# Windowed attention in units of four head pairs, with the value product turned around

## The reference

```python
x = attn_layer(shift_tokens(x), Wqkv[i], ...) + x      # 16 heads of 64
x = ffn_layer(shift_tokens(x), ...) + x
# in attn_layer
q, k, v = split(x @ Wqkv)
q, k = l2norm(q) * qs, l2norm(k) * ksc                  # then rotary tables
sim = einsum('bhwie,bhwje->bhwij', bq, bk2) * 8.0       # windows of 32, look back one window
attn = softmax(where(mask, -big, sim), -1)
out = einsum('bhwij,bhwje->bhwie', attn, bv2)
return out @ Wo
```

## Time and profile before

| what | us |
|---|---|
| median of three runs | 3748.63 (3744.89 to 3750.44) |
| the profiled execution, its own time | 3743.95 |
| its span | 3742.1 |
| TensorE busy | 3470.4 (93%) |
| VectorE busy | 3141.4 (84%) |
| ScalarE busy | 2271.7 (61%) |
| GpSimd busy | 1852.4 (50%) |

### The profile page before, as it was taken

One profiled execution on the slowest core, in us unless ns is written; L12 is line 12 of the kernel. 1 busy time (PEld: TensorE's weight loads), 2 busy tenths in 40 slices (PEclk: granted clock), 3 DMA queues, 4 the chain that ended last, 5 costly groups with the idle time before them and its releaser, 6 DMA issues.

```text
span 3742.1 us, 161812 instructions
## 1 busy us (share of the span) xinstructions
PE 3470.4 (93%) x63907; PEld 2773.6 (74%) x63907; DVE 3141.4 (84%) x6016; ACT 2271.7 (61%) x4159; POOL 1852.4 (50%) x1604
## 2 busy tenths in 40 slices
PE   5758999999999999999999999999999999999996
PEld 2326787877788878788878788877788887788784
DVE  8987888888788888788888788888788888888883
ACT  2014666666666666666666666666566666666663
POOL 2435455454554554545554445545455445455541
PEclk9988999999999999999999999999999999999998
DMA  2002423323333323333223333232432332332332
GB/s 84 9 28 50 104 60 70 77 54 78 91 67 77 72 56 80 82 77 77 64 64 76 85 77 71 57 77 67 95 72 59 73 77 54 79 74 60 70 77 73
DMA packets 186363, 261.00 MB, mean 70 GB/s; under 512 B 31670, under 2 KB 89908, under 8 KB 185396
## 3 DMA queue, kind: packets, MB, share of 16 engines
q1 hardware_dynamic: 186164, 258.24, 30.7%
HBM read 22.30 MB, written 4.19 MB: 7 GB/s over the span
## 4 chain that ended last, share of the span: by engine, by line
PE 71%; issue 13%; DVE 7%; POOL 3%; ACT 3%; SPq 2%; DMA 1%; ACTq 0%; POOLq 0%; DVEq 0%
PE bank L653 9%; PE bank L705 8%; PE bank L637 7%; PE bank L613 6%; PE obank L687 6%; PE bank L738 5%; PE bank L615 4%; PE bank L614 4%; PE bank L697 4%; PE bank L663 4%; PE bank L745 3%; DVE xs_lo L1139 3%; PE bank L647 2%; PE bank L628 2%; PE bank L630 2%
## 5 line engine op out<-in xcount | busy, mean ns | idle before, releaser
L951 POOL TENSOR_TENSOR qn<-qn,rinv 128x512 f32<-128x512 f32 x768 | 805.4, 1065 | 1382.1 <-DVE rinv L1198 1382.1
L945 POOL TENSOR_TENSOR qn<-ropec,ropes 128x512 f32<-128x512 f32 x768 | 982.9, 1294 | 274.6 <-DVE ropes L1150 230.8
L1149 DVE TENSOR_TENSOR ropec<-bank,rots 128x512 f32<-128x512 f32 x768 | 526.7, 686 | 116.0 <-ACT sq L833 63.7
L1158 DVE TENSOR_REDUCE ss<-sq 128x8 f32<-128x512 f32 x768 | 513.2, 679 | 88.0 <-ACT sq L833 82.6
L1150 DVE TENSOR_TENSOR ropes<-bank,rots 128x512 f32<-128x512 f32 x768 | 523.7, 682 | 0.0
L833 ACT ACTIVATE sq<-bank 128x512 f32<-128x512 f32 x768 | 448.8, 598 | 87.7 <-PE bank L615 68.9
L855 ACT ACTIVATE Pr<-Pr 128x512 f32<-128x512 f32 x384 | 241.9, 630 | 399.1 <-DVE Pr L1209 396.9
L637 PE MATMUL bank<-ident,qn 128*128 128x128 f32 x3072 | 464.1, 274 | 18.4 <-POOL qn L951 14.9
L653 PEld LDWEIGHTS bank<-kT,qT 64*32 64x32 f32 x24576 | 363.1, 107 | 122.0 <-issue 121.9
L613 PE MATMUL bank<-wqkv_hi,xs_hi 128*128 128x512 f32 x768 | 353.1, 460 | 99.2 <-DVE xs_lo L1139 90.8
L637 PEld LDWEIGHTS bank<-ident,qn 128*128 128x128 f32 x3072 | 375.9, 141 | 83.9 <-issue 18.8
(11 more groups left out here) (137 smaller groups left out, 6215.9 us busy)
## 6 DMA issues: line engine op xcount, KB each, us to landing
V<-Vt SPq DMA_DIRECT2D x576, 260.0 KB
V<-Vt SPq DMA_DIRECT2D x192, 130.0 KB
V<-Vt SPq DMA_DIRECT2D x192, 65.0 KB
xres<-X SPq DMA_DIRECT2D x96, 128.0 KB
X<-x SPq DMA_DIRECT2D x96, 128.0 KB, 2.0
wqkv_raw<-L_ffn_Wqkv SPq DMA_DIRECT2D x6, 1536.0 KB
xraw<-X SPq DMA_DIRECT2D x97, 64.0 KB
xraw<-X SPq DMA_DIRECT2D x97, 63.8 KB
```

The costliest lines, as they stand in the source:

```text
L945: pool.tensor_tensor(qn[:, c, :], ropec[:, c % ROPE_RING, :], ropes[:, c % ROPE_RING, :], ALU.add).then_inc(rope_sum.sem, 1)
L951: pool.tensor_tensor(heads8(qn[:, c, :]), heads8(qn[:, c, :]), rinv[:, 8 * c:8 * c + 8].unsqueeze(2).broadcast_to([P, 8, DH]), ALU.mult).t ...
L1149: dve.tensor_tensor(halves(ropec[:, c % ROPE_RING, :]), raw, table(t, 2 * kind), ALU.mult)
L1158: dve.tensor_reduce(ss[:, 8 * c:8 * c + 8], heads8(sq[:, c % 2, :]), AX.X, ALU.add).then_inc(ss_done.sem, 1)
```

## The change

1. A unit of attention is now 128 queries and four head pairs (8 heads) rather than every second head. The scores of the two heads of a pair lie in the two halves of the rows and go to two banks (`b_sim` is now the first 256 columns of both banks of `pair`); the mask matmul becomes two of 256 columns.
2. The value product has V as the stationary side, in strips of 32 of the 64 head columns, and PT as the moving side (32 columns): 64 matmuls a unit rather than 32, and its output (`b_o`, the other 256 columns of both banks) is already transposed. Step `ot` goes from TensorE; ScalarE copies `b_o` to OT.
3. The softmax sum no longer comes from a column of ones. VectorE sums Pr and takes the reciprocal (step `rs`), and GpSimd scales Pr ahead of the transpose (step `pn`). VectorE's step `pv` goes.
4. Scores and value product share the two banks, so each of them waits for the reader of the one before (`pair_free`). The freed bank makes the projection banks three.
5. The V moves are issued in two groups, 8 and 10 transfers, for the two halves of the tokens. Wo's rows are loaded in the matching order.
6. The written-out order of all four engines is new.

```diff
-V_DMAS = 10
+V_DMAS = [8, 10]
 ORDER = {
     "pe": """
-        tr.0' pt.2'' w1.0''' pv.1'' proj.0 proj.1 tr.1' ot.0'' w1.1''' tr.2' pv.2'' pt.3'' tr.3' proj.2
-        proj.3 tr.4' ot.1'' w1.2''' tr.5' pv.3'' proj.4 ot.2'' tr.6' w2.0''' ot.3'' tr.7' proj.5 proj.6
-        qk.0' wo.0'' qk.1' proj.7 v.0 mean.0'' pt.0' qk.2' var.0'' pt.1' pv.0' qk.3' v.1 v.2 ln.0'' v.3 """,
+        w1.0''' pt.1'' tr.1' proj.0 proj.1 proj.2 w1.1''' tr.2' pv.1'' tr.3' w1.2''' proj.3 proj.4 proj.5
+        tr.4' pt.2'' w2.0''' tr.5' pv.2'' tr.6' pt.3'' proj.6 tr.7' pv.3'' proj.7 qk.0' wo.0'' qk.1' v.0
+        pt.0' mean.0'' qk.2' v.1 var.0'' v.2 pv.0' v.3 ln.0'' qk.3' tr.0 """,
     "act": """
...
+        xs.0 wa.1 wa.2 tr.0' w1.0''' proj.0 tr.1' proj.1 pt.1'' w1.1''' tr.2' proj.2 ot.1'' tr.3' w1.2'''
+        wc.2''' proj.3 qk.3'' tr.4' pt.2'' proj.4 tr.5' proj.5 ot.2'' tr.6' pt.3'' proj.6 tr.7' ot.3''
+        proj.7 qk.0' x1.0'' wc.0'' v.0 pt.0' mean.0'' qk.1' v.1 ot.0' v.2 v.3 qk.2' ln.0'' wc.1'' wc.3''' """,
     "dve": """
...
+        rs.2'' xs.0 wa.1 wa.2 qk.3'' w1.0''' proj.0 sums.0 sums.1 w1.1''' proj.1 proj.2 sums.2 w1.2'''
+        proj.3 rs.3'' sums.3 w2.0''' sums.4 proj.4 proj.5 sums.5 sums.6 proj.6 qk.0' proj.7 rs.0' x1.0''
+        qk.1' sums.7 mean.0'' qk.2' var.0'' rsqrt.0 rs.1' ln.0'' """,
     "pool": """
...
+        norm.3' add.0 norm.4' norm.5' add.1 add.2 norm.6' pn.3'' norm.7' add.3 add.4 pn.0' add.5 add.6
+        norm.0 pn.1' norm.1 pn.2' add.7 norm.2 """,
 }
-        obank = ps("obank", [P, 2, 512])
-        b_proj, b_trA, b_trB, b_sim, b_c = bank[0:2], bank[2], bank[3], bank[4], bank[5]
+        pair = ps("pair", [P, 2, 512])
+        b_proj, b_trA, b_trB, b_c = [bank[0], bank[1], bank[4]], bank[2], bank[3], bank[5]
+        b_sim = pair[:, :, 0:4 * 2 * WIN]
+        b_o = pair[:, :, 4 * 2 * WIN:512]
             def b_qk(b, u):
...
+                pair_free("qk", b, u)
+                for par in range(2):
+                    pe.matmul(b_sim[:, par, :], identb[:], maskb[:, 1 if t else 0, :].unsqueeze(1).broadcast_to([P, 4, 2 * WIN]),
+                              start=True, stop=False, skip_group_check=True)
+                for j in range(4):
                     for w in range(4):
+                        for par in range(2):
+                            rows = slice(64 * par, 64 * par + 64)
+                            q0 = t * P + w * WIN
+                            mm = pe.matmul(b_sim[w * WIN:(w + 1) * WIN, par, j * 2 * WIN:(j + 1) * 2 * WIN],
+                                           qT[rows, 4 * mh + j, q0:q0 + WIN],
+                                           kT[rows, 4 * mh + j, q0:q0 + 2 * WIN],
+                                           start=False, stop=w == 3 and j == 3, skip_group_check=True)
+            def pair_free(kind, b, u):
+                at = PAIR_ORDER.index((kind, u))
+                k, n = PAIR_ORDER[at - 1]
                 batch = b if at else b - 1
+                if k == "qk":
+                    hold(pe, pe_held, sim_shift.sem, sim_shift.at(batch, n + 1))
                 else:
+                    hold(pe, pe_held, ot_copied.sem, ot_copied.at(batch, n + 1))
             def b_pv(b, u):
...
+                for w in range(4):
+                    for jj in range(2):
+                        wg = 4 * t + w
+                        for odd in range(2):
+                            j = 2 * jj + odd
+                            for dh in range(2):
+                                for par in range(2):
+                                    rows = slice(64 * par, 64 * par + 64)
+                                    strip = 32 * (2 * (par ^ odd) + dh)
+                                    mm = pe.matmul(b_o[strip:strip + 32, odd, jj * P + w * WIN:jj * P + (w + 1) * WIN],
+                                                   V[rows, wg // 2, wg % 2, 4 * mh + j, 32 * dh:32 * dh + 32],
+                                                   PT[rows, u % 2, j * P + w * WIN:j * P + (w + 1) * WIN],
+                                                   start=True, stop=True, skip_group_check=True)
-            def b_ot(b, u):
-                pe.wait_ge(on_done.sem, on_done.at(b, u + 1))
-                trB_free(b, "ot", u)
-                for j in range(4):
-                    mm = pe.transpose(b_trB[:, j * P:(j + 1) * P], On[:, u % 2, j * P:(j + 1) * P], ident[:])
-                mm.then_inc(trB_full.sem, 1)
+            def b_pn(b, u):
+                pool.wait_ge(rs_done.sem, rs_done.at(b, u + 1))
+                pool.tensor_tensor(heads8(Pr[:, u % 2, :]), heads8(Pr[:, u % 2, :]),
+                                   rs[:, u % 2, :].unsqueeze(2).broadcast_to([P, 8, 2 * WIN]), ALU.mult).then_inc(p_scaled.sem, 1)
-            def b_pv(b, u):
-                dve.wait_ge(o_full.sem, o_full.at(b, u + 1))
...
+            def b_rs(b, u):
+                dve.wait_ge(p_ready.sem, p_ready.at(b, u + 1))
+                dve.tensor_reduce(rsum[:, u % 2, :], heads8(Pr[:, u % 2, :]), AX.X, ALU.add).then_inc(rsum_done.sem, 1)
+                dve.wait_ge(rsum_done.sem, rsum_done.at(b, u + 1))
+                dve.reciprocal(rs[:, u % 2, :], rsum[:, u % 2, :]).then_inc(rs_done.sem, 1)
```

More of the change, by code:

```diff
@@ L246, in build @@
         v_copied = per_batch("v_copied", 4)
-        v_placed = per_batch("v_placed", 16 * V_DMAS)
+        v_placed = [per_batch(f"v_placed_{t}", 16 * V_DMAS[t]) for t in range(2)]
         trA_full = per_batch("trA_full", 8)
@@ L409, in load_weights @@
                 sp.dma_start(wqkv_raw[:], Wqkv[one].rearrange("l p n -> p (l n)")).then_inc(w_in_sem, 16)
-                for slot in range(2):
+                for odd in range(2):
                     for par in range(2):
-                        src = Wo[one].rearrange("l (j s r p) n -> s r p (l j) n", j=4, s=2, r=2)[slot, par]
-                        sp.dma_start(wo_raw[slot * 64:slot * 64 + 64, 4 * par:4 * par + 4, :], src).then_inc(w_in_sem, 16)
+                        src = Wo[one].rearrange("l (i o r p) n -> o r p (l i) n", o=2, r=2, p=64)[odd, par]
+                        half = 64 * (par ^ odd)
+                        sp.dma_start(wo_raw[half:half + 64, odd::2, :], src).then_inc(w_in_sem, 16)
                 sp.dma_start(w1_raw[:], W1[one].rearrange("l p n -> p (l n)")).then_inc(w_in_sem, 16)
@@ L446, in load_x, with place_v, move @@
                 sp.dma_start(xraw[64:P, 1:T], X[64:P, bass.ds(g * T, T - 1)]).then_inc(x_loaded.sem, 16)
[L448 to L468, removed]
+            def place_v(n, t):
+                hold(sp, sp_held, v_copied.sem, v_copied.at(n, 2 * t + 2))
+                hold(sp, sp_held, o_full.sem, o_full.at(n - 1, 2 * t + 2))
+                for par in range(2):
+                    half = 64 * par
+                    def move(dst, w, odd, src, rows, tile=t):
+                        d = V[dst:dst + rows, 2 * t + w, odd].rearrange("p m c -> p (m c)")
+                        v = Vt[src:src + rows, tile, par].rearrange("p m c -> p (m c)")
+                        sp.dma_start(d, v).then_inc(v_placed[t].sem, 16)
+                    move(half, 0, 1, 0, 64)
+                    move(half, 1, 1, 64, 64)
+                    move(half, 1, 0, WIN, 64)
+                    move(half + WIN, 0, 0, 0, WIN)
+                    if t == 1:
+                        move(half, 0, 0, P - WIN, WIN, tile=0)
             def body(n, g, lags, layer, c_layers, conv_c=None):
@@ L533, in _ @@
             for m in range(3):
-                mm = pe.transpose(b_sim[:, m * P:(m + 1) * P], la_w_rows[:, m, :], ident[:])
+                mm = pe.transpose(bank[4][:, m * P:(m + 1) * P], la_w_rows[:, m, :], ident[:])
             mm.then_inc(la_wt, 1)
@@ L593, in la_output @@
                 for t in range(4):
[L594 removed]
+                    mm = pe.matmul(pair[:, 1, t * P:(t + 1) * P], la_y[:, t * P:(t + 1) * P], la_w[:, 3, :], start=True, stop=True)
                 mm.then_inc(la_po.sem, 1)
@@ L640, in b_qk @@
             def b_qk(b, u):
-                t, par = UNIT[u]
+                t, mh = UNIT[u]
                 if u == 0:
                     pe.wait_ge(trA_copied.sem, trA_copied.at(b, 8))
[L645 to L649, removed]
-                    for w in range(4):
[L651 to L656, removed]
+                pair_free("qk", b, u)
[3 more added lines that the diff above has]
+                for j in range(4):
+                    for w in range(4):
+                        for par in range(2):
[5 more added lines that the diff above has]
+                                           start=False, stop=w == 3 and j == 3, skip_group_check=True)
                 mm.then_inc(sim_full.sem, 1)
             def b_pt(b, u):
-                pe.wait_ge(p_ready.sem, p_ready.at(b, u + 1))
-                trB_free(b, "pt", u)
+                pe.wait_ge(p_scaled.sem, p_scaled.at(b, u + 1))
+                pe.wait_ge(pt_copied.sem, pt_copied.at(b, u) if u else pt_copied.at(b - 1, 4))
```

(10 more changed lines are left out.)

110 lines of the change are left out of this document (47 added, 63 removed).

## The result

| kernel | median us | ratio to before, 95% interval |
|---|---|---|
| before | 3748.8 | |
| changed | 4531.6 | 1.208 (1.205 to 1.211) |

The account below looks back on a forecast made before the run. TensorE's steps, one after the other, times 96 batches plus one wait, were taken as the bound. Terms -167 - 92 + 12 + 204 - 91 + 85 = -49 us took 3744 to 3695, stated as 3690, range 3550 to 3830.

Parts of the forecast that it names:

- The value product: TensorE, turned-around product: 64 added instructions at 8.2 to 8.7 ns, +0.53 us a unit, +204 us (+115 to +346).
- Scores in eight places: TensorE, score matmuls: a unit falls from 1.03 to 0.79 us, -92 us over 384 units.
- The transposes: TensorE, line 697: the four output transposes of each unit disappear, 0.435 us each time, -167 us.
- The wait for xs_lo: TensorE, ahead of a batch's first projection: the whole 90.8 us wait is credited, -91 us (0 to -91).
- The wait for the roots: TensorE at ln.0'': new wait for the reciprocal roots, 0.85 us a batch, +85 us (0 to +150).
- The shared banks: Scores and value product wait for the previous reader; thinly covered, costed at nothing (-5 to +40 us).
- GpSimd: Four added scalings of 4.3 us raise it from 17.3 to 21.6 of 34 us a batch, just hidden.
- VectorE: Second limit: no difference in its work, 29.3 us a batch still fits in TensorE's about 34.0.
- Transfers: V moves, 10 to 18 issues a batch: up to 0.7 us late for ScalarE's copy, costed at nothing.
- A: Value product: small instructions cost 12.9 to 14.0 ns, +317 to +346 us, so 3808 to 3837 us; chance 0.18.
- B: Value product: the two row halves exclude each other in a bank, +442 instead of +204, 3933 us; chance 0.08.
- C: VectorE or the softmax chain sets the pace: waits of 0.5 us a batch, +48, back to 3743; chance 0.13.

Follow-up runs that it names:

- e7: The changed kernel with the value product in strips of 64 in units 0 and 2, of 32 in units 1 and 3: 3718.8 us, 0.993.
- e1: The changed kernel with the value product in two strips of 64 instead of four of 32, half the instructions: 3661.9 us, 0.978.
- e3: The changed kernel with each row half of the value product writing into its own bank: 4570.7 us, 1.219.
- e4: The kernel before with the value product issued twice in the last two of four units: 3932.9 us, 1.049.
- e6: The kernel before with the value product issued twice in the last three of four units: 4363.8 us, 1.165.
- e9: The code of e4 with 128 idle semaphore increments ahead of the layers: 4064.5 us, 1.083.
- e5: The kernel before with the value product issued twice by a two-turn hardware loop around one copy of its code: 4096.9 us, 1.094.

## Why the prediction was wrong

**What bounds the kernel.** "So the time is the sum of TensorE's steps, one after the other, times 96 batches, plus one wait" was right in the main for the kernel before and for the kernels here whose code is held. It is the sentence that failed for the changed one: the steps are still what I said, but TensorE is not given the instructions in time. I had no rival for it. What could have warned me stands in the page of before: q8, 138 packets, nearly all of them near the changes of layer. These are the 15 packets of 100 us there; between 1600 and 1800 us, in mid-layer, there is none:

```profile
q8 instruction: 15, 0.25, 1.1%
```

So the loop's code was held, and holding it must have a limit. My stretch of 34.55 us lay at such a change of layer, too; in mid-layer a batch takes 34.3 (from wo to wo, 1664.91 - 1630.59).

**The value product.** "I charge the 64 added instructions at 8.2 to 8.7 ns" priced their work. That was close: 1.22 us a unit where the code is held (e7, and the changed kernel between its stops) against 1.32 forecast, 38 us too dear over 384 units. What the term left out is that they are also 256 more pairs of code in the body. It is the term that failed, by some 800 us, and e1, whose body has none of them (648 pairs), gives the whole back.

**Where the 870 us between the changed kernel and e1 are.** Stops without a releaser: some 590 us against 31. Work at the low clock: the mean clock is 0.918 against 0.969. The product's own price: 0.15 us x 384 = 58 us. What is left is 870 - 559 - 58 = 253 us net. The two profiles say the same from the other side: TensorE's busy time is 3750.3 - 3376.5 = 374 us more, 316 beyond the product's own, and its idle time grows by 499 us only, since the stops cover some 60 us of waits that e1 has. I put the 316 us on the clock, which rows show at 0.50 and 0.52 behind long stops; no run separates it from the stops.

**Scores in eight places** took 0.78 us as forecast, -92 us. The masks take 0.32 us as one matmul did (1605.30 - 1604.98 in e1's timeline), so nothing instead of +12. **The transposes** are gone, -167 us. **The wait for xs_lo** is gone, -91 us, but in e1 TensorE waits 49.3 us for the copy of qT, 36 of them in five waits of 5.4 to 8.6 us at the start and at changes of layer, where I forecast nothing. So e1's batch in mid-layer is 1.5 us shorter than before, which over 96 would be 141 us, and its span only 84.5.

**The wait for the roots** was sized at 85 us. In e1 it is 36.0 us in 93 waits, the right place and less than half the size; in the changed kernel it is hidden by the stops. **The shared banks**: no wait for them reaches 3 us in all (L652 for Pr, 2.4 us). **GpSimd** and **VectorE** did not become the bound in e1. **Transfers**: ScalarE's copy of v does wait for them, 90.7 us in all in e1, and TensorE doesn't feel it.

**The rivals.** A put the loss in small instructions, but as work: it needed more than 10.3 ns for each added one, and they take (1.22 - 0.79) / 64 = 6.7 ns. B is refuted by e3. C would have been a second engine: in e1 the wait for the roots, 0.4 us in a batch, is all that comes near it. A kernel that has all four units in strips of 32 and whose code is held was not run. From e1 and e7 it can be estimated: a batch in mid-layer takes 32.85 us in e1 and 33.11 in e7 (from wo to wo in their timelines), so four such units add 2 x 0.26 x 96 = 50 us to e1, 3712 us, where I forecast 3690. But the rest of e7's 57 us lies at the changes of layer, where it fetches 24 packets more than e1; if that doubles too, four units come to 3662 + 2 x 57 = 3776 us, slower than before. So whether the changed kernel would be faster than before with its loop's code held, as I forecast, is open.

**What the page said.** The Trainium skill, "Runtime: NRT & Kernel Launch", section Instruction fetch mechanics, says that TensorE has 128 KiB for 2048 instructions, filled in 16 KiB blocks of 256, and that a taken branch to a place outside of a window of two pages forces a fetch first. The trace agrees in the packet's size and in the stop at the loop's jump. By its 2048 the changed body would fit with some 1870 recorded instructions (all that the trace has of TensorE in a batch: loads, matmuls and some 65 for semaphores, registers and the branch), and it does not: the runs put the limit lower, at 1642 recorded instructions on the edge and 1770 beyond it. By its 256 in a block, the 9 packets of a turn are an estimated 2304 instructions, the whole body and more. By its window of two pages, 512 instructions, the jump back in the kernel before (a body of 1386) would force a fetch; that kernel fetches nothing in mid-layer while its loop turns, and disagrees. The prediction did not weigh this page.

## What to carry to other kernels

Count the instructions in a hardware loop's body before and after a change, on each engine, and read the instruction queues of the page: if there are packets near the changes of layer only, the body is held, and growth costs little more than its own work up to an edge, and beyond it up to a fifth of the time. Prefer one wide matmul to two narrow ones when both take about as long. When an engine idles in mid-unit with no releaser, look at the instruction queue before you look at operands.

## What the runs showed of the hardware that I had not expected

- TensorE's loop body is held between turns at 1386 recorded instructions (before); 1642 (788 pairs, e4) hold or spill by where the body starts, and 1770 (852 pairs, e6, 772 packets) spill. Near the edge a shift by 64 or 128 instructions changes the time from 3933 to 3886 or to 4065 us, and a loop can spill in part, with two and seven packets in alternate turns (e4's last layer, e9's first five) instead of nine in each.
- Behind a stop of 2.2 or 3.4 us the granted clock was 0.50 to 0.52; behind one of 0.77 us it was 1.00.
- A hardware loop of two turns in each unit costs little code and some time: e5's unit takes 1.94 us for 130 instructions against 0.79 us for 64, 17 ns for each that is added, against 9.8 ns in e4 (1.42 us for 128), where they stand in line.
- 128 matmul instructions of 32 columns in eight places take 1.22 us (e7), 64 with 64 weight columns in four places 1.07 us (e1).
